# One wide product for the maxima, a third bank of transposed scores, and the gated weights unpacked inside the tiles

## The reference, cut to what matters

```python
def _L0_xattn_ref(q, k, v, gamma):         # q = layernorm(x), k = v = ctx; B=8, Dq=256, Lq=Lk=512
    qh = q.reshape(B, 8, 32, Lq); kh = k.reshape(B, 8, 32, Lk); vh = v.reshape(B, 8, 32, Lk)
    qk = jnp.einsum('bhdq,bhdl->bhql', qh, kh) / sqrt(32)
    sm = jax.nn.softmax(qk, axis=-1)
    return gamma * jnp.einsum('bhql,bhdl->bhdq', sm, vh).reshape(B, 256, Lq)
# x = x + that; then a gated FFN:
nib = w[:, :, None] >> shifts & 15          # w_gu: 2816 x 512 codes, dequantised
h = silu(gate) * up;  y = h @ w_down.T;  x = x + y / rms(y)
# layer 1: quantised cross attention, ternary FFN (untouched by the change)
```

## Time and profile before

| | |
|---|---|
| Time, median of 3 runs | 2071.74 us (2069.01 to 2075.08) |
| Time of the profiled execution | 2074.52 us, span in the trace 2072.8 us |
| TensorE busy | 1828.5 us, 88% of the span |
| VectorE busy | 1523.5 us, 74% |
| ScalarE busy | 1238.5 us, 60% |
| GpSimd busy | 891.3 us, 43% |
| Mean granted TensorE clock | 0.952 |

### The profile page before, as it was taken

The page is one execution under the profiler, slowest core; times in us unless marked ns, Lnnn a source line. Parts: engine busy times, 40 slices in busy tenths (PEclk is TensorE's granted clock), DMA queues, the critical chain, the costliest instruction groups (busy, mean ns, idle before and its releaser), DMA issues. The chain is left out here.

```text
span 2072.8 us, 34290 instructions
## 1 busy us (share of the span) xinstructions
PE 1828.5 (88%) x11981; PEld 831.3 (40%) x12094; DVE 1523.5 (74%) x2806; ACT 1238.5 (60%) x2016; POOL 891.3 (43%) x953
## 2 busy tenths in 40 slices
PE   4999999966999997993989999999999997579998
PEld 1333333322443433452534444444444443334443
DVE  5676777776547364886889999999999985783443
ACT  4676677543536340441449999999999993431211
POOL 5455556333326140002008888888888881000000
PEclk9999999988999998996989999999999998889999
DMA  9665442020000002110006565555655555000000
GB/s 197 183 161 120 92 105 65 6 84 1 0 1 0 0 1 71 31 30 25 0 13 107 107 109 106 109 109 106 108 108 108 108 108 198 6 1 21 21 20 21
DMA packets 318051, 143.41 MB, mean 69 GB/s; under 512 B 273872, under 2 KB 290256, under 8 KB 316752
## 3 DMA queue, kind: packets, MB, share of 16 engines
q1 hardware_dynamic: 317904, 141.50, 31.1%
HBM read 70.15 MB, written 4.19 MB: 36 GB/s over the span
## 5 line engine op out<-in xcount | busy, mean ns | idle before, releaser
L1454 ACT ACTIVATE a_prob<-a_psS,a_bias,q_scale 128x1024 uint8<-128x1024 f32 x512 | 610.2, 1211 | 27.7 <-PE a_psS L1347 24.5
L1383 DVE TENSOR_REDUCE a_tops<-a_psM 128x1 f32<-128x512 f32 x1024 | 622.8, 678 | 2.5 <-PE a_psM L1337 0.6
L1433 POOL CAST a_wide<-a_pairs 128x2048 int16<-128x2048 uint8 x256 | 481.5, 1894 | 97.1 <-DMA a_pairs<-a_prob 83.0
L1337 PE MATMUL a_psM<-KT,QO 128*128 128x512 bf16 x968 | 352.3, 387 | 15.6 <-DVE a_tops L1383 10.0
L1347 PE MATMUL a_psS<-KT,QO 128*128 128x512 bf16 x967 | 293.5, 380 | 7.0 <-ACT a_prob L1454 3.8
L1359 PEld LDWEIGHTS a_psO<-V,a_wide 128*128 128x128 f16 x4096 | 174.6, 96 | 145.2 <-DVE QO L1396 23.0
L744 POOL TENSOR_TENSOR g_sum<-g_sum 128x512 f32<-128x512 f32 x88 | 126.8, 1441 | 197.3 <-DVE g_sum L809 197.3
L458 ACT ACTIVATE prob<-psT 128x512 f32<-128x512 f32 x256 | 147.8, 598 | 89.5 <-PE psT L621 88.3
L1359 PE MATMUL a_psO<-V,a_wide 128*128 128x32 bf16 x4096 | 181.4, 177 | 20.3 <-DVE QO L1396 15.6
L918 PE MATMUL g_psY<-raw_dn,g_hT 128*128 128x512 f32 x352 | 162.3, 622 | 26.2 <-DVE raw_dn L769 15.8
L513 DVE TENSOR_REDUCE rmax<-psS 128x1 f32<-128x512 f32 x256 | 156.0, 680 | 33.6 <-PE psS L606 33.6
(11 more groups left out here) (199 smaller groups left out, 2844.2 us busy)
## 6 DMA issues: line engine op xcount, KB each, us to landing
xs<-in_x SPq DMA_DIRECT2D x64, 256.0 KB, 7.5
cs<-in_ctx SPq DMA_DIRECT2D x64, 256.0 KB, 9.7
KT<-in_w SPq DMA_DIRECT2D x2, 4096.0 KB, 22.1
raw_gu<-in_gu SPq DMA_DIRECT2D x4, 1408.0 KB, 7.1
vs<-in_ctxT SPq DMA_DIRECT2D x16, 256.0 KB, 3.0
k_cT<-in_ctxT SPq DMA_DIRECT2D x16, 256.0 KB, 2.7
a_pairs<-a_prob SPq DMA_TRANSPOSE x256, 2.7
out<-x_sb SPq DMA_DIRECT2D x16, 256.0 KB, 2.0
```

Of the source, the lines that this page charges most:

```text
L1337: pe.matmul(psM[n % NM][:, :], QOf[:, i * P:(i + 1) * P], KTf[:, keys:keys + 512], start=True, stop=True).then_inc(shown, 1)
L1383: v.reduce_max(tops[i // JOIN % NB][:, i % JOIN, c:c + 1], psM[n % NM][:, :], AX.X).then_inc(topped, 1)
L1433: pool.tensor_copy(wide[i % NV][:, :, :, :].rearrange("p k c q -> p k (c q)"), both).then_inc(widened, 1)
L1454: act.activation(prob[i % NP][:, k * HK:(k + 1) * HK], psS[g % NS][:, :], ACT.Exp, scale=q_scale[:, i:i + 1], bias=bias[i // JOIN % NB][:, ...
```

## The change

1. The four 128-column products per unit become one of 512 columns. For that `less` holds one selector per head (`[51, HT, P]`), and `mrow` holds the turned maxima four times side by side, each copy multiplied with `of_block`, which keeps only the rows of one block of queries. The copy of 51 x 128 becomes a VectorE `tensor_tensor` of 51 x 512.
2. `psM` is gone. The transposition goes to the next bank of the `psS` ring (17 places per tile instead of 16, `rows_bank`), and the first three scores of a tile wait for `mrow_ready` in place of `maxed`. The bank that becomes free is a third `psT`; a transposed score waits for the exponential of the third unit before it.
3. `raw_gu` shrinks to two groups, is loaded at tiles 2, 3, 9 and 11, and is unpacked in pieces of 704 columns: six passes (two pieces, three passes each) at the end of VectorE's steps 4, 5, 6, 7, 11, 12, 13 and 14.

```diff
+    NT3 = 3
+    NG = NU + 1
+    UP = 2
+    UNPACK = (4, 5, 6, 7, 11, 12, 13, 14)
+    FETCH_GU = (2, 3, 9, 11)
+    UW = 2 * FI // (2 * UP)
...
-        mrow = [sb(f"mrow{i}", [PARTS, P], BF16) for i in range(2)]
+        mrow = [sb(f"mrow{i}", [PARTS, LC, P], BF16) for i in range(2)]
...
-        less = sb("less", [PARTS, NU, P], BF16)
+        of_head = sb("of_head", [PARTS, HT], F32)
+        of_block = sb("of_block", [PARTS, LC], F32)
+        less = sb("less", [PARTS, HT, P], BF16)
+        raw_gu = sb("raw_gu", [P, 2, 2 * FI], I32)
...
-        psT = [pb(f"psT{i}", [P, DM], F32) for i in range(2)]
+        psT = [pb(f"psT{i}", [P, DM], F32) for i in range(NT3)]
...
-        psM = pb("psM", [PARTS, P], BF16)
...
+        def rows_bank(j):
+
+            return psS[(NG * j + NU) % 3][0:PARTS, 0:P // 2].bitcast(BF16)
...
-                if 2 <= j < 2 + CH:
-                    g = j - 2
-                    sp.dma_start(env["raw_gu"][:, g, :],
-                                 gu_in[g * P:(g + 1) * P, :]).then_inc(env["gu_loaded"][g], 16)
+                if j in FETCH_GU:
+                    g = FETCH_GU.index(j)
+                    if g >= 2:
+                        sp.wait_ge(bits_s, 6 * UP * (g - 1))
+                    sp.dma_start(raw_gu[:, g % 2, :], gu_in[g * P:(g + 1) * P, :]).then_inc(gu_loaded[g], 16)
...
-                v.tensor_copy(mrow[j % 2][:, :], psM[:, :]).then_inc(mrow_ready, 1)
+                v.tensor_tensor(mrow[j % 2][:, :, :], rows_bank(j).unsqueeze(1).to_broadcast((PARTS, LC, P)),
+                                of_block[:, :].unsqueeze(2).to_broadcast((PARTS, LC, P)),
+                                ALU.mult).then_inc(mrow_ready, 1)
...
+            def unpack(k):
+
+                g, first = k // 2, k % 2 * UP
+                base = 3 * UP * k
+                v.wait_ge(gu_loaded[g], 16)
+                cuts = [slice((first + i) * UW, (first + i + 1) * UW) for i in range(UP)]
+                for at in cuts:
+                    move_bits(v, env, raw_gu[:, g % 2, at]).then_inc(bits_s, 1)
+                for i, at in enumerate(cuts):
+                    v.wait_ge(bits_s, base + i + 1)
+                    keep_bits(v, raw_gu[:, g % 2, at]).then_inc(bits_s, 1)
+                for i, at in enumerate(cuts):
+                    v.wait_ge(bits_s, base + UP + i + 1)
+                    v.tensor_scalar(env["w_gu"][:, g, at], raw_gu[:, g % 2, at].bitcast(F32), 2.0 ** 126, None,
+                                    ALU.mult).then_inc(bits_s, 1)
...
-                if j == NT - 2:
-                    move(0)
-                    move(1)
-                    mask(0)
-                    mask(1)
-                if j == NT - 1:
-                    move(2)
-                    move(3)
-                    scale(0)
-                    scale(1)
-                    mask(2)
-                    mask(3)
-                    scale(2)
-                    scale(3)
+                if j in UNPACK:
+                    unpack(UNPACK.index(j))
...
-                if g >= 3:
+                if n >= 3:
                     pe.wait_ge(maxed, g - 2)
-                pe.matmul(psS[g % 3][:, :], qs[j % 3][:, h, c * P:(c + 1) * P], ks[j % 3][:, h, :],
+                elif j:
+                    pe.wait_ge(mrow_ready, j)
+                pe.matmul(psS[(NG * j + n) % 3][:, :], qs[j % 3][:, h, c * P:(c + 1) * P], ks[j % 3][:, h, :],
...
-                if g >= 2:
-                    pe.wait_ge(exped, g - 1)
-                out = psT[n % 2]
+                if g >= NT3:
+                    pe.wait_ge(exped, g - NT3 + 1)
+                out = psT[g % NT3]
...
-                for q in range(LC):
-                    mm = pe.matmul(out[:, q * P:(q + 1) * P], less[:, h * LC + q, :], mrow[j % 2][:, :],
-                                   start=False, stop=(q == LC - 1))
-                mm.then_inc(tscored, 1)
+                pe.matmul(out[:, :], less[:, h, :], flat(mrow[j % 2][:, :, :]), start=False,
+                          stop=True).then_inc(tscored, 1)
...
-                pe.transpose(psM[:, :], rparts[j % 2][:, :, :].rearrange("p a b -> p (a b)"), id_b[:, :]).then_inc(turned, 1)
+                pe.transpose(rows_bank(j), rparts[j % 2][:, :, :].rearrange("p a b -> p (a b)"), id_b[:, :]).then_inc(turned, 1)
```

More of the change, by code:

```diff
@@ L134, in build @@
         ffn = ctx.enter_context(ExitStack())
-        env["raw_gu"] = ffn.enter_context(nc.sbuf_tensor("raw_gu", [P, CH, 2 * FI], I32))
         env["w_gu"] = ffn.enter_context(nc.sbuf_tensor("w_gu", [P, CH, 2 * FI], F16))
-        env["gu_loaded"] = [ffn.enter_context(nc.semaphore(f"gu_loaded{g}")) for g in range(CH)]
         mix_rows(env, x_in, ctx_in, ctxT_in, gu_in)
@@ L266, in mix_rows @@
             sem(f"m_{n}") for n in ("inverted", "mixed", "added", "after", "norm_own", "bits"))
+        gu_loaded = [sem(f"m_gu_loaded{g}") for g in range(CH)]
         block = ctx.enter_context(nc.Block())
@@ L457, in exp @@
                     act.wait_ge(pv_done, g - RING + 1)
-                act.activation(prob[:, n % RING, :], psT[n % 2][:, :], ACT.Exp,
+                act.activation(prob[:, n % RING, :], psT[g % NT3][:, :], ACT.Exp,
                                scale=float(D0) ** -0.5).then_inc(exped, 1)
@@ L512, in maxima @@
                     v.wait_ge(scored, g + 1)
-                    v.reduce_max(rmax[j % 2][:, n:n + 1], psS[g % 3][:, :], AX.X).then_inc(maxed, 1)
+                    v.reduce_max(rmax[j % 2][:, n:n + 1], psS[(NG * j + n) % 3][:, :], AX.X).then_inc(maxed, 1)
                 v.wait_ge(maxed, NU * (j + 1))
@@ L585, in _ @@
             v.wait_ge(picked, 3)
-            v.tensor_scalar(less[:, :, :], pick[:, :].unsqueeze(2).to_broadcast((PARTS, NU, P)), -1.0, None,
+            v.reduce_sum(of_head[:, :], pick[:, :].rearrange("p (h c) -> p h c", c=LC), AX.X).then_inc(picked, 1)
+            v.reduce_sum(of_block[:, :], pick[:, :].rearrange("p (h c) -> p c h", c=LC), AX.X).then_inc(picked, 1)
+            v.wait_ge(picked, 5)
+            v.tensor_scalar(less[:, :, :], of_head[:, :].unsqueeze(2).to_broadcast((PARTS, HT, P)), -1.0, None,
                             ALU.mult).then_inc(picked, 1)
@@ L659, in steps @@
                     weigh(j, LC - 1)
-            pe.wait_ge(picked, 4)
+            pe.wait_ge(picked, 6)
             pe.wait_ge(masks, 11)
```

## The result

The changed kernel takes 2093.95 us (median of 4, 2091.37 to 2096.29) where the kernel before took 2072.28 beside it: ratio 1.0101, 95% interval 1.0086 to 1.0115. It is slower by about 21 us. Forecast were 2088 us and slower; the time lies 6 us above the point, inside the range and inside case A's own range. The profiled execution took 2093.24 us, 18.7 more than that of before.

What follows compares the result with a forecast made beforehand. VectorE was taken to pace each tile's first six steps, TensorE and ScalarE the tail. Terms summed to +16.3 us: 2090.8 on the profiled scale, 2088 us beside the 2071.7 median; range 2074 to 2100.

Steps and rivals of the forecast that it cites:

- case A: All terms come as worked out: 2088 us, own range 2080 to 2096, chance 0.57.
- The wide product: One 512-column product for four narrow ones per unit saves 0.009 us, taken as -1.5 us.
- The third bank: Tile tail: fourteenth unit no longer waits for the twelfth exponential, 0.65 us earlier in fourteen tiles, -9.1 us.
- `mrow`: Tile head, before the maxima: longer VectorE instruction, 0.61 for 0.14 us, net +0.40 in tiles 1 to 13, +5.2 us.
- Tile 0 and the old falls of the clock: Fourth unit's 2.44 us wait in tile 0 shortened, -1.9 us; clock falls after three 0.81 us waits gone, -3.5 us.
- The passes: Heads of six tiles (steps 4 to 7, 11, 12): unpacking fully exposed before the maxima, 3.2 us each, +19.2 us.
- The clock in the stalls: After six new TensorE stalls, half clock for some two steps, 1.2 us each, +7.2 us (bounds 0 and 10).
- Step 13: Passes behind step 13, with no statistics there: VectorE's 2.67 us of idle time is used, leaving +1.0 us.
- rival D: Stronger stalls: VectorE and GpSimd slow each other (first mechanism, +6), clock falls repeatedly per stall (+5); 2099 us, chance 0.13.
- The tail: Last tiles: only 0.27 us of the unpacking was exposed there, so taking it away gives -0.3 us.
- B: First form: clock stays up in stalls, 2081 us; second: wide product hides one weight load, 2079 us; chance 0.22.
- C: Both weight loads hidden beside the single product, unit 0.44 for 0.64 us, turning earlier; 2064 us, chance 0.08.

Runs made afterwards that it cites:

- the bank alone: Kernel before with only the third `psT` bank and the turned maxima in the `psS` ring: 2055.20 us, ratio 0.9919.
- the first experiment: Changed kernel with the unpacking put back into the last two tiles, in 2816-column passes over four loaded groups: 2059.9 us, ratio 0.9939.
- three: Changed kernel plus twelve unused 512-column TensorE products in front of the score that stalls behind the passes: 2076.56 us, ratio 1.0018.
- the fourth experiment: Changed kernel with the six short passes moved one place earlier, between the reciprocals and the `mrow` instruction: 2085.08 us, ratio 1.0050.
- five: Changed kernel with the six short passes directly behind the maxima, in front of the reciprocals: 2055.90 us, ratio 0.9917.
- second experiment: Kernel before with only the unpacking moved into the tiles, as in the changed kernel: 2107.93 us, ratio 1.0166.

## Why the prediction was right, and which terms were off

Case A came true: parts 1 and 2 a gain of about ten us, the unpacking a larger loss. Term by term, inside the mixing stage:

- **The wide product**, forecast -1.5 (0.009 per unit). The distance stayed 0.32. Tiles 1 and 2, in which the longer `mrow` instruction costs nothing, became 0.74 us shorter each; the bank alone makes them 0.67 shorter, so the wide product gives 0.07. Right. The 131 ns per 512-column product that the page "TensorE: Matmul & The Clock Gate" of the Trainium skill gives in the section "Back-to-back issue gap" would have misled: behind a 512-column product with 128 weight columns no next product starts sooner than 0.21 us in any trace here.
- **The third bank**, forecast -9.1 (0.65 in 14 tiles). The wait of the fourteenth unit is gone, and periods of the bank alone are 22.93 for 23.60: 0.67. Right, though tile 14 gained no more than 0.2.
- **`mrow`**, forecast +5.2 (0.61 us for 0.14 at the head, +0.40 net). The next instruction stands 0.61 behind it (181.91, 182.52); regular tiles are 23.34 for 23.60, so of the 0.74 gained 0.48 goes back. It does so in the eleven tiles from 3 to 13 and not in 1 and 2: 5.3 in all. Part 1 as a whole was forecast +3.7 and measured +4.2.
- **Tile 0 and the old falls of the clock**, forecast -1.9 and -3.5. Tile 0 gained 4.2: the 2.44 us wait of rows 5 is gone, and so is the clock fall that lay between 58 and 64 us in the trace of before (granted clock 0.86 and 0.57 in stretches of 3 us). The other two old falls went too: tiles 5 and 10 had taken 25.19 us, 1.6 more than their neighbours. The edits of the experiments one, three, four and five don't reach tile 0, and it took 25.3 to 27.7 us in their traces, so its 4.2 is uncertain by some 1 us.
- **The passes**, forecast +19.2 (six times 3.2). The six passes take 2.73 us in each of the six heads; TensorE kept busy gives 2.73 per tile. So +16.4: the share that I had added for GpSimd was too much in these heads, and the 2.9 worked out from VectorE's own rows was the better value.
- **The clock in the stalls**, forecast +7.2 (six times 1.2). This is the term that was mis-sized: the clock's part is 2.5 to 3.4 us in each of the six, some 17. The level was right (0.50), and so was the pace of a step at that level (1.9 forecast, 1.94 measured, against 1.21). What failed is "for some two steps", for which the prediction gives no row: at 0.73 us lost per step, 2.5 to 3.4 us are three and a half to four and a half steps. The falls in the kernel before last 3.4 us each, about two such steps; here the clock stayed at 0.50 for 6.8 us in four of the six tiles and for 10.2 in two, with TensorE busy nearly throughout. Why it took that long is not shown by any run. The length of the stall alone doesn't set it: behind the same stall of 2.21 us in the fourth experiment the clock stayed low for 3.4 us in two tiles, 6.8 in three and 10.2 in one.
- **Step 13**, forecast +1.0. VectorE's 2.67 us of idle time were used as I said, but the passes took 4.27 us (397.98 to 402.25), since the first two took 2.61 for 1.06 while GpSimd worked beside them, and the stall behind them (1.86 us) brought a clock fall of its own, 0.50 from 403.0 to 409.8. Together +4.3, of which the clock is 2.2. That VectorE and GpSimd hold each other up is rival D's first mechanism, in one tile of seven.
- **The tail**, forecast -0.3 for the work taken out of the last tiles, measured -2.2. The forecast read ScalarE's input as ready at 422.92 in a tile where the clock had fallen (a `weigh` at 405.08 with 1.93 us for 1.06) and ScalarE was late by it. Without a fall the input is ready 1.5 us sooner with two banks (second experiment) and 2 us with three, and VectorE's long passes stand out: the first experiment and the third bank alone have no fall in tile 15 and take 37.02 us all the same.

The terms of the unpacking (passes, step 13, tail, new falls) were forecast +27.1. Measured as the difference of the two kernels that differ in nothing else they are 35.8 inside the stage and 34 in the medians. The others were forecast -10.8 and measured -12.4. That the point came within 6 us is in part luck: inside the +35.8, the passes' 2.8 and the tail's 1.9 too high hide the clock's 9.7 and step 13's 3.3 too low. The rest of the near hit is the second error, which took back 1.6.

*The rivals.* B's first form, a clock that stays up, is what the twelve added products bring about: 2076.6 us, for the 2081 that I had worked out. B's second form and C, a smaller distance with the wide product, didn't happen with 51 rows. That the 0.1 us is a weight load that is not hidden, as the prediction has it, no run shows; shown is that it goes with the change of the row count. Of D, the hold-up with GpSimd came in one place, and the clock fell once in each stall and not more often, but cost more than D's 5 us. The time lies in A's range, but part of the way there is D's. The page "TensorE: Matmul & The Clock Gate" of the Trainium skill says in the section "Why this matters for your kernels" that pauses send the clock to its low level. The traces agree: 0.50 after a pause of 3.08 us, in each of the six tiles with passes in their heads, and in the kernel before also after 0.81 us.

## What to carry to other kernels

Before moving work into a loop, look for the engine's idle time that lies *behind* the work others wait for, not for the tile's free time in sum: the same passes cost 34 us in front of the maxima and nothing directly behind them. Price a stall of TensorE with the slower clock that follows it, here as much again as the stall; and check what GpSimd does beside each place where VectorE's copies and scalings may go. Where two products alternate with 0.1 us more than usual on both sides of one of them, compare the row counts of their weights before merging or reordering anything.

## What the runs showed of the hardware that I had not expected

- The distance between 512-column products is 0.32 us on both sides of one whose weights have 51 or 64 rows between such with 128, and 0.22 when all have 128, f16 beside bf16. With four narrow products the distances before the first and behind the fourth are longer by 0.1 us too, while between the four, all of 51 rows, there are 0.056 us. Without it each tile is 1.1 us shorter.
- VectorE's scalings over 704 or 2816 columns and GpSimd's products hold each other up: 2.89 us for 0.95, 13.92 for 1.27; VectorE's maxima, which read PSUM, show no such stretch beside GpSimd (0.66 to 0.69 us each, before and after).
- Once TensorE's clock had fallen to 0.50 in a head, it stayed there for 6.8 or 10.2 us with TensorE busy nearly all of that time, while behind the 0.81 us waits of before it took 3.4.
